# Attention beside experts on one core: two buffers of moved keys, filled at step 12 of the sequence before, and a different order in step 0

## The chip, the core and the metric

The kernel runs as one program on one core of a Trainium2 chip. The metric is device time in microseconds (us) of one execution, from the first to the last instruction and what lies around them. Every engine of the core (TensorE, VectorE, ScalarE, GpSimd, SyncE) runs an instruction stream of its own, and the streams meet at semaphores. In the profile TensorE is PE (its weight loads are PEld), VectorE DVE, ScalarE ACT, GpSimd POOL, and SyncE, which issues nearly all DMAs here, SP.

## What is computed

The input x has 8 sequences of 512 tokens with 512 features. Both stages are residual, with a layer norm before and after:

```python
x = x + layernorm(attention(layernorm(x)))
x = x + layernorm(experts(layernorm(x)))
```

Attention has 16 heads of 32 features for the queries and **one** head of keys and values that all of them share; it is causal, with biases:

```python
q = (h @ q_w.T + q_b).reshape(b, s, 16, 32)
k = h @ k_w.T + k_b                      # 32 features, shared by the 16 heads
v = h @ v_w.T + v_b
scores = einsum('bqhd,bkd->bhqk', q, k) / 32 ** 0.5      # then causal mask and softmax
out = einsum('bhqk,bkd->bqhd', attn, v).reshape(b, s, 512) @ o_w.T + o_b
```

The expert stage sends each token to 2 of 8 experts (gated, 352 features inside) and adds a shared expert (1408 features inside) under a sigmoid gate.

## The kernel before, in words

`build_layer` runs four parts one after another: `build_attention`, `build_routing`, `build_experts` (tokens sorted into places of 256) and `build_shared`. The change touches `build_attention` alone.

**Precision.** Products are made from pairs of float32r tiles, a high part and the rest (`low`), so a product of 512 features takes 12 matmuls (`split_product`, L400: 4 chunks by 3 passes). For the scores the parts are stacked along the contraction: `Qs` holds 3*32 rows per head (high, low, high of the queries), `KsS` the matching 96 rows of the keys (high, high, low) of one sequence. A second copy of the keys, `KsT`, has one more row of ones, so that the product with row 97 of `Qs`, the negated maxima, comes out shifted for the exponential.

**Order of the work.** There is no planner; each engine has its order written out in a function `turn(b)`, which handles sequence b in 16 steps s, one head of queries per step, in a software pipeline with lags. In step s of turn b TensorE does, in this order (L597 to L614):

- `query_scores(b, s)` (L423): four score products of head s against `KsS` and the mask (L434, L438) in three PSUM units. Before unit u it waits until DVE has reduced the head before to its maxima (`max_ready`). In step 0 it also waits for `kS_moved`, and in steps 0, 4, 8, 12 for `q_moved`.
- `rows_of_maxima(b, s)` (L579): transposes the maxima of the head before (L421). ACT copies the row out (`take_row`, L880) and SP moves it by DMA into row 97 of `Qs` (`move_row`, L343).
- `first_filler(b, s)` (L501): other dense work in the one bank `F_ps`. The chunks of the projected queries of sequence b+1 are made in steps 12, 13 and 15, chunk 3 in step 0 of the next turn (`Q_STEP`, L274). Other steps hold the output projection, the transposes of the input and the router.
- `begin_values` / `end_values`: products of the exponentials with ones or values (L458), a group of four heads at a time.
- `key_scores(n, h)` (L441, matmuls L451), two heads behind: transposed shifted scores against `KsT`, unit by unit, each waiting until ACT has taken the same unit of the head before (`pt_ready`). In steps 1 and 14 it stands before the values, in the others behind them.

**Step 0 is an exception**: `first_filler(b, 0)`, the projection of query chunk 3 (L403), stands ahead of `query_scores(b, 0)`. DVE mirrors it: it takes the low part of the filler's product (`low_q`, L637) before the third unit of maxima, as in the steps of `PAIRED` (2, 3, 9, 10); in all others after it.

ACT, in step s: exponentials of unit 0 of head s-3 (L869), `take_row`, the high part of a mixed group (L913), exponentials of units 1 and 2, the filler's high part (`high_q`, L837), then normalizations; steps 0 and 1 hold two each of `xn2` (L819) from b = 2 on. `high_q` precedes `low_q` of the same chunk; the next filler may begin when `low_q` is done (`qkv_lo`).

SP, in step s: from step 15 the first thing is the refill of `KsS` for sequence b+1: wait for `scores >= 3*H*(b+1)`, which is the last score product of sequence b, then three DMAs from `vk_h` (`move_k`, L320, issues L322), then `move_row`. `vk_h` itself is made in step 11 (`low_vk`, L624: ACT L828, DVE L630 and L632). `KsT` is moved in step 2 of turn b+1.

**Turns.** `turns` (L291) writes out turns 0 and 1, loops over 2 to 5 with a register (`Fori`), and writes out 6 to 9; the last two have no new sequence and drain the pipeline. Before turn 0 the first keys and chunks 0 to 2 of the queries are projected; chunk 3 of sequence 0 is made in step 0 of turn 0.

Of the kernel before, what the change touches and what calls it, by code (L numbers as in the profile page):

```python
# [26 lines left out]
P = 128  # L27
# [151 lines left out]
def build_attention(nc, x, wq, wvk, wo, wr, qb, vkb, ob, x1_out, xn_out, xnT_out, logits, idf, idb, mask, norm_constants):  # L179

    ctx = ExitStack()
    with ctx:
# [25 lines left out]

        QK = 3 * HD
        Qs = sb("Qs", [QK + 1, H, S], F32R)  # L210
        KsS = sb("KsS", [QK, S], F32R)
        KsT = sb("KsT", [QK + 1, S], F32R)
        V = sb("V", [P, QT, HD])
        ones_f = sb("ones_f", [P, QT, HD])
# [76 lines left out]
        block = ctx.enter_context(nc.Block())  # L291

        def turns(engine, turn):
            turn(0)
            turn(1)
            with engine.Fori(2, NB - 2) as b:
                turn(b)
            for b in range(NB - 2, NB + 2):
                turn(b)

        def seq(dram, b):
            return dram[bass.ds(b, 1)].rearrange("o p t d -> p (o t) d")
# [2 lines left out]
        def _(sp):  # L305
# [27 lines left out]
            sp.wait_ge(xT1_ps, C)  # L333
            sp.dma_start(x_in[:], seq(x, 1)).then_inc(x_in_s, 16)
            sp.wait_ge(qkv_lo, 1)
            move_k(0, KsS, kS_moved)
            move_k(0, KsT, kT_moved)
            spill_q(0, 0)
            spill_q(0, 1)
# [8 lines left out]
                    sp.dma_start(Qs[QK:QK + 1, h, :].bitcast(F32),  # L348
                                 row[:, h % 2, :].bitcast(F32)).then_inc(row_moved[h % 2], 16)

            def turn(b):
                for s in range(H):
                    if s == H - 1 and has(b + 1):
                        sp.wait_ge(scores, 3 * H * (b + 1))
                        move_k(b + 1, KsS, kS_moved)
                    move_row(b, s)
                    if s == 0 and has(b):
                        spill_q(b, 2)
                    if s == 1 and has(b):
                        move_q(b, 2)  # L360
                        spill_q(b, 3)
                    if s == 2 and has(b):
                        if has(b - 1):
                            sp.wait_ge(shifted, 3 * H * b)
                            move_k(b, KsT, kT_moved)
                        move_q(b, 3)
                    if s == 4 and has(b - 2):
                        sp.wait_ge(xT2_lo, C * (b - 1))
                        for half in range(2):
                            sp.dma_start(xnT_out[bass.ds(b - 2, 1), half].rearrange("o p c t -> p (o c) t"),  # L370
                                         xT[half][:].bitcast(F32)).then_inc(xnT_stored, 16)
                        sp.dma_start(seq(xn_out, b - 2), xn2[:]).then_inc(xn2_moved, 16)
                    if s == 6 and has(b - 1):
                        if has(b - 2):
                            sp.wait_ge(x1_ready, QT * (b - 1))
                        sp.dma_start(x_res[:], seq(x, b - 1)).then_inc(x_res_s, 16)
                    if s == 11 and has(b + 2):
                        sp.wait_ge(xT1_ps, C * (b + 2))
                        sp.dma_start(x_in[:], seq(x, b + 2)).then_inc(x_in_s, 16)
                    if s == 13 and has(b + 1):  # L380
                        spill_q(b + 1, 0)
                    if s == 14:
                        if has(b + 1):
                            move_q(b + 1, 0)
                            spill_q(b + 1, 1)
                        if has(b - 1):
                            sp.wait_ge(x1_ready, QT * b)
                            sp.dma_start(seq(x1_out, b - 1), y[:]).then_inc(x1_stored, 16)
                    if s == 15 and has(b + 1):
                        move_q(b + 1, 1)  # L390
# [7 lines left out]
        def _(pe):  # L398
# [21 lines left out]
                pe.wait_ge(max_ready, 3 * (H * n + h) + 3)  # L420
                nc.tensor.matmul(AV_ps[0:QT, 0:P], nmax[:, h % 2, :], idr[:], start=True, stop=True).then_inc(rows_ps, 1)  # L421

            def query_scores(b, s):  # L423
                if s == 0:
                    pe.wait_ge(kS_moved, 48 * b + 48)
                if s % HG == 0:
# [2 lines left out]
                for units in ((0,), (1, 2)):  # L429
                    for u in units:  # L430
                        if has(n):
                            pe.wait_ge(max_ready, 3 * (H * n + h) + u + 1)
                        for i, col in S_UNITS[u]:
                            nc.tensor.matmul(S_ps[u][:, col:col + (i + 1) * P], Qs[0:QK, s, i * P:(i + 1) * P],  # L434
                                             KsS[:, 0:(i + 1) * P], start=((i, col) == S_UNITS[u][0]), stop=False)
                    for u in units:
                        (i, col), k = S_UNITS[u][0], len(S_UNITS[u])
                        nc.tensor.matmul(S_ps[u][:, col + i * P:col + (i + k) * P], idb[:, 0, :],  # L438
# [155 lines left out]
                        pe.wait_ge(row_taken, H * head(b, s, 2)[0] + head(b, s, 2)[1] + 1)  # L594
                    transpose_maxima(n, h)

            def turn(b):  # L597
                for s in range(H):
                    if s == 0:
                        first_filler(b, s)  # L600
                    if has(b):
                        query_scores(b, s)
                    rows_of_maxima(b, s)
                    if s > 0:
                        first_filler(b, s)
                    n, h = head(b, s, 2)
                    if s in (1, 14) and has(n):
                        key_scores(n, h, head(b, s, 3))
# [10 lines left out]
        def _(dve):  # L619
# [168 lines left out]
                    if (s, at) == (15, 0):  # L788
                        x1_.guess(b - 1)

            def turn(b):
                for s in range(H):
                    maximum(b, s, 0)
                    norm_steps(b, s, 0)
# [1 line left out]
                    maximum(b, s, 1)  # L796
                    norm_steps(b, s, 1)
                    spread_inverses(b, s)
                    if s in PAIRED or s == 0:
                        first_low(b, s)  # L800
                        maximum(b, s, 2)
                        norm_steps(b, s, 2)
                        second_low(b, s)
                    else:
                        maximum(b, s, 2)
                        norm_steps(b, s, 2)
                        first_low(b, s)
# [8 lines left out]
        def _(act):  # L816
# [95 lines left out]
                        act.wait_ge(projected, QT * n)  # L912
                    nc.scalar.activation(OT[0][:, g, :], mixed_f[:], ACT.Copy).then_inc(OT_hi, 1)  # L913

            def turn(b):
                for s in range(H):
                    exponentials(b, s, 0)
                    take_row(b, s)
# [24 lines left out]
        def _(pool):  # L943
# [44 lines left out]
                pool.wait_ge(y_normed, QT * n + i + 1)  # L988
                nc.gpsimd.tensor_tensor(y[:, i, :], y[:, i, :], x_res[:, i, :], ALU.add).then_inc(x1_ready, 1)

            def turn(b):
                for s in range(H):
                    if s == 6 and has(b + 1):
                        norm[0].refine(b + 1)
# [849 lines left out]
```

## Time and profile before

| | us |
|---|---|
| median of 3 runs (lowest, highest) | 2149.88 (2144.54, 2150.34) |
| the profiled execution, its own time | 2153.74 |
| its span, first to last instruction | 2152.0 |
| PE busy in the span | 1973.5 (92%) |
| PEld, DVE, ACT, POOL busy | 1568.8, 1129.8, 781.6, 478.2 |
| mean granted TensorE clock | 0.943 of full |

The profiled execution is 3.9 us longer than the median of the three runs; its span is 1.7 us short of its own time. A row of a timeline has the start, the duration, the engine, line and operation, what is written from what, the shape and the count of merged instructions; in brackets, the idle time of the engine just before and what ended it. A "busy" matmul row shows that PE was occupied, not that it ran at its peak. [...]

### The profile page before, as it was taken

The page shows a single profiled execution, that of the slowest core. Times are in us where ns is not written, and L with a number is a line of the kernel's source. Part 1 is how long each engine was busy: PE and PEld are TensorE (multiplying, and loading weights), DVE is VectorE, ACT ScalarE, POOL GpSimd, SP SyncE. Part 2 cuts the span into 40 slices and gives each one's busy share as a digit, 9 for nine tenths or more (in the row PEclk, how much of TensorE's full clock was granted, in tenths as well). Part 3 has the DMA queues.
Part 4 walks back from the last instruction along what each step waited for, and adds up shares of the span by engine and source line. Part 5 has one row for each costly group of instructions (what it writes and reads, how often), then busy time and mean ns, then how long its engine had stood idle before and what let it go on. Part 6 is the DMA issues. An engine that isn't in the chain of part 4 may idle for free. (4 is left out here: it accounts for less than half of the span.)

```text
span 2152.0 us, 34973 instructions
## 1 busy us (share of the span) xinstructions
PE 1973.5 (92%) x11932; PEld 1568.8 (73%) x11932; DVE 1129.8 (52%) x2478; ACT 781.6 (36%) x1576; POOL 478.2 (22%) x1087
## 2 busy tenths in 40 slices
PE   5989999999999743899999999999999999999995
PEld 3665656656565422799999999978888888888884
DVE  4556656666565328677777657643433324333243
ACT  3445545455453410466666546432111111111111
POOL 1223324234241320211111112001113021130212
PEclk9799999999999765899999989999999999999998
DMA  5144353442533132566666657632123020230202
GB/s 173 51 114 127 117 174 106 147 143 109 176 98 126 50 113 95 195 237 236 235 235 235 240 188 268 243 113 69 37 81 118 19 97 31 86 117 19 97 24 94
DMA packets 114453, 281.47 MB, mean 131 GB/s; under 512 B 11680, under 2 KB 26272, under 8 KB 105024
## 3 DMA queue, kind: packets, MB, share of 16 engines
q1 hardware_dynamic: 103328, 244.18, 32.9%
q0 software_dynamic: 11040, 36.18, 5.0%
q8 instruction: 51, 0.84, 0.2%
q14 instruction: 34, 0.28, 0.0%
HBM read 198.79 MB, written 78.12 MB: 129 GB/s over the span
## 5 line engine op out<-in xcount | busy, mean ns | idle before, releaser
L1257 PE MATMUL ex_bank<-ex_xT,ex_gu 128*128 128x256 f32 (+12 forms) x2808 | 358.0, 284 | 1.0 <-DVE ex_xT L1421 1.0
L1257 PEld LDWEIGHTS ex_bank<-ex_xT,ex_gu 128*128 128x128 f32 (+1 forms) x2808 | 344.1, 185 | 4.9 <-issue 1.4
L1289 DVE TENSOR_TENSOR sh_silu<-sh_silu,sh_bank 128x512 f32<-128x512 f32 x88 | 60.6, 688 | 457.4 <-ACT sh_silu L1282 451.1
L1282 ACT ACTIVATE sh_silu<-sh_bank 128x512 f32<-128x512 f32 x88 | 52.6, 598 | 591.4 <-PE sh_bank L1257 546.1
L1257 PE MATMUL sh_bank<-sh_xT,sh_gate 128*128 128x512 f32 x1056 | 256.2, 392 | 5.2 <-DVE sh_dn L1704 5.2
L677 DVE TENSOR_REDUCE at_nmax<-at_bank 128x1 fp32r<-128x384 f32 (+3 forms) x512 | 222.6, 476 | 61.2 <-PE at_bank L438 60.7
L1269 PE MATMUL sh_bank<-sh_dn,sh_act 128*128 128x512 f32 x1056 | 254.3, 390 | 0.0
L1257 PE MATMUL sh_bank<-sh_xT,sh_up 128*128 128x512 f32 x1056 | 253.7, 389 | 0.0
L1257 PEld LDWEIGHTS sh_bank<-sh_xT,sh_gate 128*128 128x128 f32 x1056 | 199.8, 189 | 47.3 <-issue 5.6
L869 ACT ACTIVATE at_PT<-at_bank 128x512 f32<-128x512 f32 (+1 forms) x384 | 184.2, 506 | 125.7 <-PE at_bank L451 101.0
L1269 PEld LDWEIGHTS sh_bank<-sh_dn,sh_act 128*128 128x128 f32 x1056 | 197.6, 188 | 43.7 <-DVE sh_act L1298 2.9
L1257 PEld LDWEIGHTS sh_bank<-sh_xT,sh_up 128*128 128x128 f32 x1056 | 198.4, 188 | 41.3
L1269 PE MATMUL ex_bank<-ex_dn,ex_act 128*128 128x512 f32 (+1 forms) x666 | 165.2, 401 | 0.6 <-issue 0.6
L451 PE MATMUL at_bank<-at_Qs,at_KsT 97*128 97x512 f32 (+3 forms) x512 | 127.1, 363 | 27.4 <-ACT at_PT L869 18.5
L1269 PEld LDWEIGHTS ex_bank<-ex_dn,ex_act 128*128 128x128 f32 (+1 forms) x666 | 124.7, 192 | 27.7 <-issue 1.5
L973 POOL TENSOR_SCALAR_AFFINE_SELECT at_PT<-at_PT 128x384 f32<-128x384 f32 x128 | 66.9, 522 | 294.4 <-ACT at_PT L869 294.3
L1349 DVE TENSOR_TENSOR ex_gu<-ex_gu_in,ex_gu 128x704 fp32r<-128x704 f32 x156 | 131.3, 884 | 1.2 <-PEq L1018 0.6
L451 PEld LDWEIGHTS at_bank<-at_Qs,at_KsT 97*128 97x128 f32 x512 | 86.7, 203 | 58.3 <-ACT at_PT L869 22.5
L434 PE MATMUL at_bank<-at_KsS,at_Qs 96*128 96x384 f32 (+3 forms) x512 | 123.0, 349 | 6.8 <-DVE at_nmax L677 5.7
L1345 ACT ACTIVATE ex_gu<-ex_gu_in 128x704 fp32r<-128x704 f32 x156 | 115.5, 801 | 27.2 <-DMA ex_dn_in<-dn_in 27.2
L1289 DVE TENSOR_TENSOR ex_silu<-ex_silu,ex_bank 128x256 f32<-128x256 f32 (+15 forms) x117 | 45.9, 392 | 142.9 <-ACT ex_silu L1282 142.8
L403 PE MATMUL at_bank<-at_xT,at_wq 128*128 128x512 f32 x384 | 95.5, 398 | 9.7 <-DVE at_q_h L637 9.2
(228 smaller groups left out, 2653.8 us busy)
## 6 DMA issues: line engine op xcount, KB each, us to landing
ex_gu_in<-gu_in SPq DMA_DIRECT2D x39, 1408.0 KB
at_Qs<-q_dram SPq DMA_DIRECT2D x96, 256.0 KB, 4.0
ex_dn_in<-dn_in SPq DMA_DIRECT2D x39, 512.0 KB
ys<-sh_yk SPq DMA_DIRECT2D x35, 512.0 KB, 2.9
q_dram<-at_q_h SPq DMA_DIRECT2D x64, 256.0 KB, 3.2
xnT<-at_xT SPq DMA_DIRECT2D x16, 1024.0 KB, 5.0
sh_xT<-xnT SPq DMA_DIRECT2D x16, 1024.0 KB
at_x_in<-x_in SPq DMA_DIRECT2D x8, 1024.0 KB, 5.1
```

The costliest lines, as they stand in the source:

```text
L403: last = nc.tensor.matmul(out, w[i][:, c, cols], xT[j][:, c, :], start=(n == 0), stop=(n == 3 * C - 1))
L434: nc.tensor.matmul(S_ps[u][:, col:col + (i + 1) * P], Qs[0:QK, s, i * P:(i + 1) * P], KsS[:, 0:(i + 1) * P], start=((i, col) == S_UNITS[u] ...
L451: last = nc.tensor.matmul(T_ps[tb][:, col:col + w], KsT[:, j * P:(j + 1) * P], Qs[:, h, j * P:S], start=((j, col) == tiles[0]), stop=((j, ...
L677: last = nc.vector.tensor_reduce(nmax[:, s % 2, i:i + 1], S_ps[u][:, col:col + (i + 1) * P], AX_X, ALU.max, negate=True)
L869: nc.scalar.activation(PT[g % 2][:, h % HG, TFROM[tb]:TFROM[tb] + TW[tb]], T_ps[tb][:, 0:TW[tb]], ACT.Exp).then_inc(pt_ready, 1)
L973: nc.gpsimd.affine_select(out=diagonals, in_=diagonals, compare_op=ALU.is_ge, fill=0.0, base=0, pattern=[[0, QT - 1], [1, P]], channel_mul ...
L1257: last = self.nc.tensor.matmul(self.gate_up_ps[c % 2][which][0:m, 0:w], cols(i, k), self.xT[j][:, k, 0:w], start=(step == 0), stop=(step = ...
L1269: last = self.nc.tensor.matmul(self.out_ps[i][:], self.act[c % 2][j][0:m, i * P:(i + 1) * P], weights(k), start=(c == 0 and step == 0), st ...
L1282: nc.scalar.activation(silu[c % 2][0:m, 0:w], gate_up_ps[c % 2][0][0:m, 0:w], ACT.Silu).then_inc(s["silu_ready"], 1)
L1289: nc.vector.tensor_tensor(silu[c % 2][0:m, 0:w], silu[c % 2][0:m, 0:w], gate_up_ps[c % 2][1][0:m, 0:w], ALU.mult).then_inc(s["product"], 1)
L1345: self.nc.scalar.activation(self.piece(q, r, 0), self.piece(q, r), ACT.Copy).then_inc(self.hi, 1)
L1349: self.nc.vector.tensor_tensor(self.piece(q, r, 1), self.piece(q, r), self.piece(q, r, 0).bitcast(F32), ALU.subtract).then_inc(self.lo, 1)
```

## The change

`KsS` becomes two buffers, used by the sequence's parity r. SP no longer fills one in step 15 behind the last scores; it fills the other one in step 12, behind that step's `move_row` and a wait for `low_vk(b+1)`. In step 0 PE does the scores and the row of maxima first and the projection of query chunk 3 after them, as in the other steps, and DVE takes all three units of maxima before `low_q`. The parity must be known when the program is written, so the loop now holds two turns in its body: turns 0 and 1 are written out, `Fori(1, 3)` runs turns (2, 3) and (4, 5), and 6 to 9 are written out.

```diff
-        KsS = sb("KsS", [QK, S], F32R)
+        KsS = [sb(f"KsS{r}", [QK, S], F32R) for r in range(2)]
...
         def turns(engine, turn):
-            turn(0)
-            turn(1)
-            with engine.Fori(2, NB - 2) as b:
-                turn(b)
+            turn(0, 0)
+            turn(1, 1)
+            with engine.Fori(1, NB // 2 - 1) as pair:
+                turn(2 * pair, 0)
+                turn(2 * pair + 1, 1)
             for b in range(NB - 2, NB + 2):
-                turn(b)
+                turn(b, b % 2)
...
-            move_k(0, KsS, kS_moved)
+            move_k(0, KsS[0], kS_moved)
...
-            def turn(b):
+            def turn(b, r):
                 for s in range(H):
-                    if s == H - 1 and has(b + 1):
-                        sp.wait_ge(scores, 3 * H * (b + 1))
-                        move_k(b + 1, KsS, kS_moved)
                     move_row(b, s)
+                    if s == 12 and has(b + 1):
+                        sp.wait_ge(qkv_lo, 5 * b + 6)
+                        move_k(b + 1, KsS[1 - r], kS_moved)
...
                             nc.tensor.matmul(S_ps[u][:, col:col + (i + 1) * P], Qs[0:QK, s, i * P:(i + 1) * P],
-                                             KsS[:, 0:(i + 1) * P], start=((i, col) == S_UNITS[u][0]), stop=False)
+                                             KsS[r][:, 0:(i + 1) * P], start=((i, col) == S_UNITS[u][0]), stop=False)
...
-            def turn(b):
+            def turn(b, r):
                 for s in range(H):
-                    if s == 0:
-                        first_filler(b, s)
                     if has(b):
-                        query_scores(b, s)
+                        query_scores(b, s, r)
                     rows_of_maxima(b, s)
-                    if s > 0:
-                        first_filler(b, s)
+                    first_filler(b, s)
...
-                    if s in PAIRED or s == 0:
+                    if s in PAIRED:
                         first_low(b, s)
```

## Rows read from the trace of the kernel before

**Rows 1.** The windows view, the attention part: window, length, busy of PE, PEld, DVE, ACT, POOL, then PEclk, DMA share, GB/s.
```profile
40.00:764.00 724.00, 672.55 (x4804) 439.39 (x4803) 432.10 (x1016) 333.48 (x727) 235.11 (x610) 0.94 0.38 122
```
**Rows 2.** The waits view, PE from 44 to 764: total us, times, longest.
```profile
PE at_bank L403 <- DVE at_q_h L637: 6.8, 7, 1.0
PE at_bank L451 <- DMA at_KsT<-at_vk_h: 5.8, 7, 1.4
```
**Rows 3.** Timeline of PE from turn 4 into turn 5.
```profile
461.38 0.81 PE L451 MATMUL at_bank<-at_Qs,at_KsT 97*128 97x512 f32 x4
463.18 3.06 PE L403 MATMUL at_bank<-at_xT,at_wq 128*128 128x512 f32 x12 [1.00 <-DVE at_q_h L637]
466.07 0.40 PE L434 MATMUL at_bank<-at_KsS,at_Qs 96*128 96x384 f32 x2
...
466.97 0.45 PE L451 MATMUL at_bank<-at_Qs,at_KsT 97*128 97x512 f32 x1
468.05 0.67 PE L451 MATMUL at_bank<-at_Qs,at_KsT 97*128 97x128 f32 x3 [0.63 <-ACT at_PT L869]
...
470.00 0.38 PE L434 MATMUL at_bank<-at_KsS,at_Qs 96*128 96x256 f32 x1 [0.68 <-DVE at_nmax L677]
...
470.78 0.49 PE L451 MATMUL at_bank<-at_Qs,at_KsT 97*128 97x512 f32 x1 [0.20 <-ACT at_PT L869]
```
**Rows 4.** Timeline of ACT at the same place.
```profile
461.65 0.69 ACT L837 ACTIVATE at_q_h<-at_bank,at_qb 128x512 fp32r<-128x512 f32 x1 [1.29 <-PE at_bank L403]
...
467.25 0.27 ACT L880 ACTIVATE at_row<-at_bank 4x128 fp32r<-4x128 f32 x1 [4.43 <-PE at_bank L421]
...
468.17 0.66 ACT L837 ACTIVATE at_q_h<-at_bank,at_qb 128x512 fp32r<-128x512 f32 x1
...
470.15 0.57 ACT L869 ACTIVATE at_PT<-at_bank 128x512 f32<-128x512 f32 x1
```
**Rows 5.** Timeline of DVE: the low part of query chunk 2, in step 15.
```profile
462.38 0.75 DVE L637 SCALAR_TENSOR_TENSOR at_q_h<-at_bank,at_qb,at_q_h 128x512 fp32r<-128x512 f32 x1 [2.26 <-ACT at_q_h L837]
```
**Rows 6.** The same view, step 11 of turn 4.
```profile
442.06 0.68 DVE L632 TENSOR_TENSOR at_vk_h<-at_vk,at_vk_h 64x512 fp32r<-64x512 f32 x1
```
**Rows 7.** Timeline of SP's issues in turn 4: steps 12 and 13, then 14, then 15.
```profile
443.39 3.97 SPq L348 DMA_DIRECT2D at_Qs<-at_row  x2
...
454.63 1.27 SPq L330 DMA_DIRECT2D at_Qs<-q_dram  x3
...
458.69 3.03 SPq L322 DMA_DIRECT2D at_KsS<-at_vk_h  x3
```
**Rows 8.** The tile view of KsS, time from issue to landing of its 24 DMAs.
```profile
DMA to landing us min/median/max: 2.0/4.5/5.3
```
**Rows 9.** Timeline of PE from turn 0 into turn 1.
```profile
114.22 3.02 PE L403 MATMUL at_bank<-at_xT,at_wq 128*128 128x512 f32 x12 [0.92 <-DVE at_q_h L637]
...
122.33 0.67 PE L451 MATMUL at_bank<-at_Qs,at_KsT 97*128 97x128 f32 x3 [0.55 <-ACT at_PT L869]
```
**Rows 10.** Timeline of PE at the start of turn 0.
```profile
39.64 3.00 PE L403 MATMUL at_bank<-at_xT,at_wq 128*128 128x512 f32 x12 [2.43 <-DVE at_q_h L637]
43.69 0.47 PE L434 MATMUL at_bank<-at_KsS,at_Qs 96*128 96x384 f32 x2 [1.04 <-DMA at_Qs<-q_dram]
...
47.05 0.25 PE L421 MATMUL at_bank<-at_idr,at_nmax 128*4 128x128 f32 x1
```
**Rows 11.** Timeline of PE: the same 32 value matmuls in step 1 of turns 4 and 7.
```profile
385.55 2.36 PE L458 MATMUL at_bank<-at_PT,at_ones_f 128*32 128x512 f32 x32
...
648.11 4.50 PE L458 MATMUL at_bank<-at_PT,at_ones_f 128*32 128x512 f32 x32
```
**Rows 12.** The windows view, steps 15 to 1 around turn 7, columns as in rows 1.
```profile
636.00:652.00 16.00, 13.72 (x74) 8.11 (x76) 4.83 (x10) 7.54 (x15) 5.65 (x21) 0.80 0.73 216
```
**Rows 13.** The DMA view, queue of instruction packets (count, MB): 298 to 570 (in the loop), 576 to 700.
```profile
q8 instruction: 2, 0.03, 0.1%
...
q8 instruction: 7, 0.11, 0.4%
```

More of the change, by code:

```diff
@@ L421, in transpose_maxima, with query_scores @@
                 nc.tensor.matmul(AV_ps[0:QT, 0:P], nmax[:, h % 2, :], idr[:], start=True, stop=True).then_inc(rows_ps, 1)
-            def query_scores(b, s):
+            def query_scores(b, s, r):
                 if s == 0:
@@ L789, in norm_steps, with turn @@
                         x1_.guess(b - 1)
-            def turn(b):
+            def turn(b, r):
                 for s in range(H):
@@ L913, in high_mixed, with turn @@
                     nc.scalar.activation(OT[0][:, g, :], mixed_f[:], ACT.Copy).then_inc(OT_hi, 1)
-            def turn(b):
+            def turn(b, r):
                 for s in range(H):
@@ L989, in add_residual, with turn @@
                 nc.gpsimd.tensor_tensor(y[:, i, :], y[:, i, :], x_res[:, i, :], ALU.add).then_inc(x1_ready, 1)
-            def turn(b):
+            def turn(b, r):
                 for s in range(H):
```

## The prediction

> **What bounds the kernel now.** I read the windows by stage first. In the attention part PE is busy 672.6 of 724 us at a mean granted clock of 0.94 [rows 1]: TensorE sets the pace there, and what is to be won is its 51 idle us and the time at the lower clock. No other engine is above 61%. The part after it starts when attention ends, so what attention saves should pass to the end whole. Then the waits of PE: two of its groups come once per turn, 6.8 us on `low_q` in 7 waits of at most 1.0, and 5.8 us on the move of `KsT` in 7 waits [rows 2]. The change is about the first, so I read the timelines from turn 4 into turn 5.
>
> The reader is to see four stops of PE there [rows 3]. The key scores of head 13 end near 462.2 (461.38+0.81). The projection of chunk 3 begins at 463.18, 1.00 late, because it waits for `low_q` of chunk 2, which ends at 463.13 [rows 5]. The scores of head 0 start only at 466.07. The row of maxima of head 15 thus reaches ACT late: ACT has been idle 4.43 before `take_row` at 467.25 [rows 4]. Behind that copy stand exponentials of head 13, so PE stops 0.63; `low_q` of chunk 3 stands ahead of a maximum on DVE, so PE stops 0.68 at 470.00; then 0.20 at 470.78, where the key scores of head 15 wait for ACT [rows 3].
>
> **The new order of step 0, PE, DVE and ACT.** From the key scores of head 13 on, with durations of these rows. The scores and the row take 0.90 (466.07 to 466.97), so they run 462.2 to 463.1, in the hole before 463.18. They need three things. The maxima of head 15, reduced in step 15, are there. The queries: their three DMAs are issued at 454.63 to 455.9 [rows 7]; even with the longest landing of a move of keys, 5.3 [rows 8], that is 461.2. The keys are discussed below. The projection starts where it did, 463.18, and ends its issue at 466.07. ACT takes the row early, in its 4.43 us of idleness, and does the exponentials of head 13 there; the 0.63 stop goes. All maxima of head 0 are done before `low_q`; the 0.68 stop goes. PE then does the key scores of head 14 (0.81) and the scores and row of head 1 (0.90) by 467.8.
>
> **What is late next** is ACT. `high_q` of chunk 3 can begin when the projection ends (463.18+3.06=466.24), instead of at 468.17 behind the copy and the exponentials. Behind it stand two normalizations and the exponential of head 14, unchanged. From `high_q` to the key scores of head 15 it was 470.78-468.17=2.61 [rows 3, 4]; now 466.24+2.61=468.85. PE waits about 1.0 there, in one piece, and the gain is 470.78-468.85=**1.9**. The norm's factors from GpSimd come early enough: nothing there follows this order. This holds for the six boundaries into turns 2 to 7: 6*1.9=11.3. Into turn 1 there are no such normalizations: scores in the hole, projection at 114.22 as before, its issue ends 117.1, key scores and scores to 118.8, then the copy and two exponentials (1.1 from the row to the second unit, as 466.89 to 468.05); the second unit starts near 119.9 instead of 122.33 [rows 9]: 2.4. Together **-13.7**. After step 1 PE is full again and every later chain (the row to SP, `KsT`) hangs on PE's own steps, so the shift stays. The KsT wait stays too: its DMAs follow the row of head 1.
>
> **The second buffer and SP.** The three moves go from step 15 (458.69 to 461.7, landed up to 5.3 later, 466) [rows 7, 8] to step 12. Without this the new order would wait for them. In step 12 they follow the row at 443.39 and a wait for `low_vk`, done at 442.06+0.68=442.7 [rows 6, 7], so SP waits for nothing. The three issues hold SP up to 3.0 us; the next row comes 3.4 us after the first (two rows span 3.97, one takes 0.6) and is needed a step later (724/128=5.7 us): cost 0. Were the first cover gone, that row would be late by at most 3.0, less than the step. In step 15 the row of head 14 goes some 2 us earlier; it was not waited for. `KsT` moves as before. DMA traffic is the same. The added buffer costs space only. PE's reads of either buffer cost the same.
>
> **The start.** Here the old order was the better one. The projection of chunk 3 ran at 39.64 while the first queries were on their way, and the scores began at 43.69, waiting for them [rows 10]. Now the scores begin at 43.69 and the projection lies bare behind them. The row of head 0 came at 47.05; now 43.69+0.90+2.89+0.90=48.4, a loss of 1.4, if the clock stays up. But PE is then idle from 37.2 to 43.7 instead of 2.4 and 1.0. After such a stop the clock may be at its lower level, where the same 32 matmuls take 4.50 us against 2.36 [rows 11], 1.9 times. Then it is 1.9*4.7=8.9, ending at 52.6, a loss of 5.6. SP's moves of chunk 2 stand behind this row, so the loss is passed on. I take **+4.0**, nearer to the low clock, since so long a stop precedes; ends 1.4 and 5.6.
>
> **The loop.** The body has two turns. In 272 us inside the loop two packets of 16 KB of instructions are fetched, in 124 us of written-out turns seven [rows 13]: the body now stays in the engines' memories and its return costs nothing that is seen. A body twice as long may not stay. It would then be fetched as the written-out turns are, which show no stop at fetches, except that the one return (turn 3 to 4) jumps to code that is not there. No row prices such a jump; the nearest is the landing of a small DMA, 2.0 to 5.3 [rows 8]. Ends 0 and 5.3, taken **+2.0**, once, because PE no longer has a hole at that place.
>
> [...]
>
> **The clock.** [...] There the 32 value matmuls cost 4.50 instead of 2.36 [rows 11], so all six cost at most 6*2.1=12.8. The change takes PE's idle time at a boundary from 2.5 (1.00+0.63+0.68+0.20) to about 1.0, and leaves that in one piece. One boundary, into turn 4, kept its clock with the same stops. So the fall is a near thing, and I take half of it away: **-6**; ends 0 and -12.8.
>
> **Sum**: -13.7+4.0+2.0-6=-13.7. Against the profiled execution, 2153.7 becomes 2140.0 (span 2138.3). That execution is 3.9 above the median of the runs shown; against the median 2149.9 becomes **2136.2**.
>
> **Rivals.**
> - *The clock holds everywhere* (0.15): all of the 12.8 returns and the start costs 1.4, the loop 0: -13.7+1.4-12.8=-25, 2125. For it: PE's density at a boundary becomes that of other steps. Against: the 1.0 in one piece.
> - *The gain is given back at the start and to the clock* (0.15): start 5.6, return 5.3, clock nothing: -2.8, 2147. For it: six of seven falls at present.
> - *The change does not do what it says* (0.04): scores in step 0 find another late input, queries or the mask unit, and the hole stays: 2149 to 2151. Against it: the landing worked out above.
> - *Slower: fetching code* (0.04). With a doubled body every one of the five engines jumps to code it does not hold, and they stand in a chain (PE, DVE, ACT, SP, back to PE), so the stops add up. Five of 5.3 are 26; with clock 0 and start 4.0 it is -13.7+4.0+26=+16, 2166. It decides from about 16 us of fetching stops. Against: in written-out turns fetches hide.
>
> **The numbers.** About 0.3%, 6.4 us, is what a measurement of this kernel can tell from no change. The forecast with its own range of 2129 to 2143 has 0.62 and is faster; the clock rival too (0.15); of the second rival 0.02. Faster 0.79, same 0.17, slower 0.04. The range, 2125 to 2148, leaves out the slower rival and the tails.
>
> **What would show it.** In the profile after: at a boundary the scores of head 0 directly behind the key scores of head 13; ACT's wait before `take_row` gone; no PE wait on DVE maxima there, and one of about 1.0 on ACT exponentials before the key scores of head 15. The L403 wait on `low_q` shrinks from 6.8 to under 1. At the start the projection lies behind 43.7. More instruction packets between turns 2 and 5; a stop of several engines at the return from turn 3 to 4. It is wrong if the boundaries keep their length, or the start costs over 6, or the granted clock is low in places where it was full.

## The result, and the profile after

| | before | after |
|---|---|---|
| median (lowest, highest), us | 2150.34 (2144.54, 2154.41) | 2138.74 (2135.79, 2139.76) |
| runs of each | 7 | 7 |
| the profiled execution, own time | 2153.74 | 2135.84 |
| its span | 2152.0 | 2134.1 |
| mean granted clock of TensorE | 0.943 | 0.949 |

The ratio is 0.9946, with a 95% interval of 0.9933 to 0.9960: 11.6 us faster, where 2136.2 was forecast. The two profiled executions lie 17.9 apart, since that of before is 3.4 above its median and that of after 2.9 below. Another 1.6 us of the 17.9 is scatter ahead of attention: the first store of queries is issued at 34.95 before and at 33.37 after.

The page of after, its first lines and its instruction queues:

```profile
span 2134.1 us, 34901 instructions
PE 1957.1 (92%) x11932; PEld 1566.4 (73%) x11932; DVE 1128.9 (53%) x2478; ACT 782.0 (37%) x1576; POOL 478.4 (22%) x1087
q8 instruction: 69, 1.13, 0.2%
q14 instruction: 50, 0.41, 0.1%
```

The windows view over the attention part, where PE's busy time was 672.55 at a clock of 0.94 [rows 1]:

```profile
40.00:764.00 724.00, 663.40 (x4828) 442.04 (x4828) 437.36 (x1031) 336.83 (x731) 242.87 (x628) 0.95 0.39 122
```

PE is busy 9.2 us less over a few more matmuls, and in the whole span 16.4 us less over the same 11932: the same work took less time. The waits of PE from 44 to 764 (total us, times, longest):

```profile
PE at_bank L452 <- ACT at_PT L867: 19.9, 19, 5.0
PE at_bank L452 <- DMA at_KsT<-at_vk_h: 6.5, 7, 1.4
PE at_bank L435 <- issue: 3.6, 1, 3.6
PE at_bank L452 <- DMA at_Qs<-at_row: 3.4, 2, 2.8
```

The group of 6.8 us on `low_q` [rows 2] is gone, the wait for `KsT` has stayed, and a single wait of 3.6 on "issue" is new. The timeline of PE from turn 5 into turn 6 is that of [rows 3], one turn later:

```profile
542.57 0.81 PE L452 MATMUL at_bank<-at_Qs,at_KsT 97*128 97x512 f32 x4
543.21 0.40 PE L435 MATMUL at_bank<-at_KsS,at_Qs 96*128 96x384 f32 x2
...
544.37 3.02 PE L404 MATMUL at_bank<-at_xT,at_wq 128*128 128x512 f32 x12
547.23 0.81 PE L452 MATMUL at_bank<-at_Qs,at_KsT 97*128 97x512 f32 x4
...
550.15 1.21 PE L452 MATMUL at_bank<-at_Qs,at_KsT 97*128 97x512 f32 x4 [1.22 <-ACT at_PT L867]
```

The scores of head 0 follow the key scores of head 13 at once, and of the four stops one of 1.22 is left. From the key scores of head 13 to those of head 15 it is 550.15-542.57=7.58 us, against 470.78-461.38=9.40 [rows 3]: 1.82 less. This stretch is called the boundary below; without its stop it takes 7.58-1.22=6.36. ACT at the same place:

```profile
544.31 0.27 ACT L878 ACTIVATE at_row<-at_bank 4x128 fp32r<-4x128 f32 x1 [0.29 <-PE at_bank L422]
...
547.43 0.69 ACT L835 ACTIVATE at_q_h<-at_bank,at_qb 128x512 fp32r<-128x512 f32 x1 [2.11 <-PE at_bank L404]
548.02 1.51 ACT L817 ACTIVATE at_xn<-at_y,at_bias_x,at_rstd_x 128x512 f32<-128x512 f32 x2
549.43 0.58 ACT L867 ACTIVATE at_PT<-at_bank 128x512 f32<-128x512 f32 x1
```

Its wait ahead of `take_row` fell from 4.43 [rows 4] to 0.29. Now it waits 2.11 for the projection, and the two normalizations stand between `high_q` and the exponential that PE wants.

**The clock behind the boundaries** is read from windows of 16 us that begin at the key scores of head 15 (columns as in rows 1, the clock third from the end). Before, into turns 1, 2, 3, 5 and 7:

```profile
122.00:138.00 16.00, 13.34 (x127) 7.30 (x128) 8.07 (x18) 4.75 (x12) 3.55 (x7) 0.89 0.56 145
205.00:221.00 16.00, 14.84 (x116) 7.46 (x120) 8.82 (x19) 7.64 (x18) 2.06 (x5) 0.79 0.57 158
295.00:311.00 16.00, 14.90 (x126) 7.24 (x124) 8.69 (x18) 7.58 (x17) 2.82 (x6) 0.81 0.54 144
...
470.00:486.00 16.00, 14.76 (x128) 7.21 (x128) 9.56 (x21) 8.27 (x19) 3.15 (x6) 0.89 0.58 157
...
645.00:661.00 16.00, 13.99 (x100) 7.32 (x101) 7.68 (x18) 6.78 (x15) 1.54 (x4) 0.74 0.58 160
```

After, at the same five places:

```profile
122.00:138.00 16.00, 13.23 (x143) 7.58 (x147) 10.31 (x23) 5.43 (x14) 3.73 (x8) 1.00 0.57 145
201.00:217.00 16.00, 14.05 (x139) 7.54 (x140) 9.84 (x22) 8.94 (x20) 3.58 (x7) 1.00 0.56 145
286.00:302.00 16.00, 13.79 (x124) 7.44 (x124) 9.42 (x19) 7.88 (x18) 3.55 (x7) 0.89 0.56 145
...
463.00:479.00 16.00, 13.76 (x124) 7.20 (x124) 9.59 (x20) 8.05 (x19) 3.58 (x7) 0.89 0.57 146
...
634.00:650.00 16.00, 14.75 (x145) 8.53 (x145) 8.92 (x19) 8.85 (x20) 3.58 (x7) 1.00 0.57 145
```

The other two boundaries read 1.00 (turn 4) and 0.89 (turn 6) before, and 1.00 and 1.00 after. In windows of 1 us the clock reads 1.00 or 0.50, but for those in which it changes (before, into turn 2: 1.00 in each from 200 to 205, 0.50 in each from 206 to 211). So a mean of 0.89 over 16 us is (1-0.89)*16/0.5=3.5 us at the lower level. Over the seven windows that makes 31.7 us before and 7.0 after. At the return from turn 3 to 4 after has a fall of its own, ahead of its window: from 366 to 382 the mean is 0.79, 6.7 us, of which some 1.4 lie under PE's stop there. These windows begin behind the boundary and do not show a fall inside it.

**The start of turn 0**, PE, against [rows 10]:

```profile
42.02 0.77 PE L435 MATMUL at_bank<-at_KsS,at_Qs 96*128 96x384 f32 x2 [6.36 <-DMA at_Qs<-q_dram]
...
43.66 4.87 PE L404 MATMUL at_bank<-at_xT,at_wq 128*128 128x512 f32 x12
...
50.75 0.50 PE L435 MATMUL at_bank<-at_KsS,at_Qs 96*128 96x384 f32 x2 [1.33 <-DVE at_nmax L675]
```

PE stands 6.36 in one piece, and the projection behind it takes 4.87 instead of 3.00. **The return of the loop** from turn 3 to 4, PE and then ACT:

```profile
369.90 0.79 PE L435 MATMUL at_bank<-at_KsS,at_Qs 96*128 96x384 f32 x2 [3.57 <-issue]
...
371.71 4.67 PE L404 MATMUL at_bank<-at_xT,at_wq 128*128 128x512 f32 x12
...
369.27 0.60 ACT L867 ACTIVATE at_PT<-at_bank 128x512 f32<-128x512 f32 x1 [2.78 <-issue]
```

Between 280 and 550 the first instruction queue moves 18 packets, 0.29 MB, where two were moved inside the loop before [rows 13], and the second 15, 0.12 MB. One of the first and two of the second lie inside PE's stop, from 366.33 to 369.90. The boundary at the return takes 13.61 us (365.52 to 379.13) where the others take 7.5 to 7.6: 3.57 for the stop, and some 2.5 for the work that ran at the lower clock.

**Where the time went**, from one issue of SP to the same one a turn later (the store of x in step 14): before 89.05, 89.24, 86.55, 88.12, 87.32, 87.41 us; after 84.82, 86.15, 90.78, 87.11, 84.09, 79.38. Five intervals are shorter by 1.0 to 8.0. The third holds the return and is 4.2 longer. The sum is 527.69 against 512.33, 15.4 less. From the last store of attention to the end it is 1370.6 before and 1370.3 after: all of the gain is in attention, as was forecast.

### The profile page after: what moved, and what is told of

The parts are those of the page before. It is cut to its first block and busy times, and to the rows that moved or that the text cites. A ratio compares the mean times of both kernels' runs of the same rounds, so it can differ in the third digit from the quotient of the medians.

```text
span 2134.1 us, 34901 instructions
## 1 busy us (share of the span) xinstructions
PE 1957.1 (92%) x11932; PEld 1566.4 (73%) x11932; DVE 1128.9 (53%) x2478; ACT 782.0 (37%) x1576; POOL 478.4 (22%) x1087
## 5 line engine op out<-in xcount | busy, mean ns | idle before, releaser
L452 PE MATMUL at_bank<-at_Qs,at_KsT 97*128 97x512 f32 (+3 forms) x512 | 120.9, 353 | 30.4 <-ACT at_PT L867 19.9
L166 POOL TENSOR_TENSOR sh_t<-sh_t 128x4 f32<-128x4 f32 x40 | 8.0, 200 | 433.1 <-DVE sh_t L153 430.6
```

Source lines behind the costliest of these rows:

```text
L166: self.nc.gpsimd.tensor_tensor(out, in0, in1, op).then_inc(self.newton, 1)
L452: last = nc.tensor.matmul(T_ps[tb][:, col:col + w], KsT[:, j * P:(j + 1) * P], Qs[:, h, j * P:S], start=((j, col) == tiles[0]), stop=((j, ...
```

## The experiments

**Everything written out.** The loop goes, and with it the return; the order of step 0 is after's.

```diff
-            turn(0, 0)
-            turn(1, 1)
-            with engine.Fori(1, NB // 2 - 1) as pair:
-                turn(2 * pair, 0)
-                turn(2 * pair + 1, 1)
-            for b in range(NB - 2, NB + 2):
+            for b in range(NB + 2):
                 turn(b, b % 2)
```

> The changed kernel with all ten attention turns written out, so that no engine jumps back; nothing else differs. Theory (the 3.57 us stop of TensorE and the 2.78 us stop of ScalarE at the return from turn 3 to 4, which the profile puts down to issue, are the fetch of code that is no longer held, and the fall of the clock behind it comes from this stop): both stops are gone, no attention boundary is longer than the others, and the time falls by 3.6 for the stop and up to 3 more for the clock, to 2132 to 2135. Rival (the stop is something else that happens once at this place, such as a late DMA or a register wait): it stays, and the time stays at 2138 to 2140. Second rival (written-out code pays at each fetch): small stops appear in turns 2 to 5 and eat the gain.

Measured: 2135.06 (2133.78 to 2137.90), ratio 0.9932 (0.9915 to 0.9950). No wait of PE or ACT on issue is left in attention. The waits of PE there:

```profile
PE at_bank L447 <- ACT at_PT L862: 19.8, 19, 4.9
...
PE at_bank L447 <- DMA at_KsT<-at_vk_h: 4.0, 7, 1.4
```

The intervals are 83.68, 85.53, 83.92, 85.62, 85.76, 81.42: in sum 6.4 shorter than after's. The part behind attention, from its last store of x to the end, gives 5 of that back (1375.3 against 1370.3); by the ratios 0.0014, 3 us, are left of it. A turn with no fall of the clock behind its boundary takes 83.7 to 83.9, one with a fall of 3.5 us (a window of 0.89) 85.5 to 85.8: the fall costs about 1.8. The 5 us behind attention were not expected; later experiments come back to them.

**The old start.** Only in the first step of all, PE takes the projection first again.

```diff
                 for s in range(H):
+                    first_ever = s == 0 and isinstance(b, int) and b == 0
+                    if first_ever:
+                        first_filler(b, s)
                     if has(b):
                         query_scores(b, s, r)
                     rows_of_maxima(b, s)
-                    first_filler(b, s)
+                    if not first_ever:
+                        first_filler(b, s)
```

> The changed kernel with one exception: in step 0 of turn 0 TensorE makes the projection of query chunk 3 ahead of the scores, as before the change. Theory (the new order loses 4 us at the start because the projection no longer lies under the arrival of the first queries): the row of maxima of head 0 comes 2 to 4 us earlier, and the time falls by 3 to 4, to about 2135. Rival (the loss is only moved: the first turn is limited by the DMAs of queries and rows, which wait for nothing of this): the time stays within 1 us of 2138.7.

Measured: 2133.04 (2131.78 to 2136.72), ratio 0.9926 (0.9908 to 0.9944), which is 0.0020 or 4.3 us below after's ratio. By the two profiles, from the first store of queries to the first store of x it is 153.05 us instead of 156.89: 3.8 less. The start had cost 3.8 to 4.3.

**The order alone**, in before: one buffer, keys moved in step 15, loop of one turn.

```diff
                 for s in range(H):
-                    if s == 0:
-                        first_filler(b, s)
                     if has(b):
                         query_scores(b, s)
                     rows_of_maxima(b, s)
-                    if s > 0:
-                        first_filler(b, s)
+                    first_filler(b, s)
```

(DVE's `if s in PAIRED or s == 0` becomes `if s in PAIRED`.)

> The kernel before with the new order of step 0 alone (TensorE and VectorE); one buffer of moved keys, filled in step 15, and the loop of one turn. Theory (the second buffer is what lets the scores run in the hole): the scores of head 0 now wait for the keys, which land near 4 us after the key scores of head 13 end; TensorE stops 3 to 4 us at each of seven boundaries, of which the new order gives back 1.9, so the time is 5 to 15 us above the kernel before, with the start loss of 4 in it: 2160 to 2175. Rival (the keys land early enough, and the buffer was not needed): it equals the changed kernel less the stop at the return, near 2134.

Measured: 2152.28 (2148.03 to 2155.56) over 12 runs, ratio 1.0008 (0.9996 to 1.0021). PE's wait group, its timeline into turn 4, and the clock from 385 to 401:

```profile
PE at_bank L434 <- DMA at_KsS<-at_vk_h: 17.1, 6, 3.9
...
377.00 0.60 PE L434 MATMUL at_bank<-at_KsS,at_Qs 96*128 96x384 f32 x2 [3.62 <-DMA at_KsS<-at_vk_h]
...
378.62 3.92 PE L403 MATMUL at_bank<-at_xT,at_wq 128*128 128x512 f32 x12
...
385.00:401.00 16.00, 14.71 (x144) 8.17 (x145) 9.88 (x21) 8.89 (x20) 3.57 (x7) 1.00 0.55 144
```

The wait for the keys comes, six times and 2.0 to 3.9 long, and takes the gain away: the early move is what the order needs. But hardly a loss followed, and the expected time was far too high. The six boundaries into turns 2 to 7 take 71.8 us together, against 56.2 before, 15.6 more: 17.1 of waits for keys, 7.2 of waits for ACT, 38.2 of work (6*6.36), and 9.3 that the work runs longer. The start costs its 4; the boundary into turn 1 gives 2.7. What pays for most of this is the clock behind the boundaries. In windows of 16 us from the key scores of head 15 all six read 1.00, where the same six had 28.2 us at the lower level before, worth 14.1. But the clock has not stayed up: it falls inside each boundary. The projection right behind each wait is slow (3.92 to 4.56 in the six places, for 3.0). In windows of 1 us around that at 377.00 the granted clock is 1.00 during the whole wait, then 0.62, 0.50, 0.50 and 0.68 from 377 to 381, and 1.00 again. So each of the six has one fall of 3.4 us, all of it on work, and the 9.3 is its price. The sum is 15.6+4.0-2.7-14.1=2.8, and measured by the ratio is 1.7 (-0.9 to 4.5).

**Buffers and loop alone.** After's two buffers and its loop of two turns, with the old order and the keys moved in step 15.

```diff
-        KsS = sb("KsS", [QK, S], F32R)
+        KsS = [sb(f"KsS{r}", [QK, S], F32R) for r in range(2)]
...
-            with engine.Fori(2, NB - 2) as b:
-                turn(b)
+            with engine.Fori(1, NB // 2 - 1) as pair:
+                turn(2 * pair, 0)
+                turn(2 * pair + 1, 1)
```

> The changed kernel with the old order of step 0 and the keys moved in step 15 as before; what is left of the change is two buffers and the loop with two turns in its body. Theory (a body of two turns is fetched anew and its one return stops TensorE and ScalarE for the fetch): one stop with the releaser issue at the return from turn 3 to 4, some 1 us shorter than in the changed kernel because 1.0 us was idle there anyway, and a time 2 to 6 us above the kernel before, 2152 to 2156. Rival (the stop belongs to the new order, whose scores follow at once): no such stop, and the time of before, 2150.

Measured: 2150.86 (2146.33 to 2153.97) over 12 runs, ratio 1.0009 (0.9995 to 1.0022). PE's waits and the return:

```profile
PE at_bank L404 <- issue: 3.6, 1, 3.6
...
373.25 5.48 PE L404 MATMUL at_bank<-at_xT,at_wq 128*128 128x512 f32 x12 [3.57 <-issue]
```

The stop of 3.57 belongs to the loop of two turns, whatever the order, and again one instruction packet of the first queue and two of the second lie inside it, from 369.68 to 373.25. Here it swallows one old stop of 1.0. The boundary at the return takes 14.45 us instead of 9.41, 5.0 more, while by the ratio the whole is only 1.9 longer (-1.1 to 4.7). In the profiled execution, the fastest of the twelve, the clock fell behind only three boundaries besides the return, where before's profile has six; why is open. Two buffers bring nothing by themselves.

**The order alone, seen from the other side.** The written-out program has the two buffers and the move in step 12; this takes from it only the order, on PE and DVE.

```diff
                 for s in range(H):
+                    if s == 0:
+                        first_filler(b, s)
                     if has(b):
                         query_scores(b, s, r)
                     rows_of_maxima(b, s)
-                    first_filler(b, s)
+                    if s > 0:
+                        first_filler(b, s)
```

> Two buffers, the keys moved in step 12, all turns written out, but the old order of step 0 on TensorE and VectorE. Theory (moving the keys earlier is worth nothing by itself, SP's three issues in step 12 are free, and written-out turns cost nothing): the boundaries show the four stops of before, 1.0, 0.63, 0.68 and 0.20, and the time is that of before, 2148 to 2152. Rival (part of the gain comes from the earlier move, since SP is free in step 15 and the landing traffic is away from the boundary): the time lies 3 or more below before, under 2147.

Measured: 2154.44 (2153.22 to 2158.31) over 12 runs, ratio 1.0031 (1.0019 to 1.0043). The old stops stand in it as they did:

```profile
374.23 3.01 PE L399 MATMUL at_bank<-at_xT,at_wq 128*128 128x512 f32 x12 [0.92 <-DVE at_q_h L633]
...
380.93 0.38 PE L430 MATMUL at_bank<-at_KsS,at_Qs 96*128 96x256 f32 x1 [0.69 <-DVE at_nmax L673]
```

The time was expected at that of before and is 0.0031, 6.6 us, above it. Most of that is the 5 us that this program, written out like the first, loses behind attention (1375.4 from the last store of x). Against the written-out program with the new order (0.9932) the order is worth 0.0099, 21 us, net of its loss at the start. So the early move alone gives nothing, the order alone gives nothing, and the two together some 25 us at seven boundaries. 13.3 of them are the stops (six boundaries of 9.29 became 7.52, and the first, 8.84, became 6.15). The clock has the rest: in windows of 16 us from the key scores of head 15, the seven boundaries read 0.89, 0.79, 0.79, 0.79, 0.89, 0.89, 0.79 with the old order (37 us at the lower level) and 1.00, 1.00, 0.89, 1.00, 0.89, 0.89, 0.89 with the new (14 us).

**A hint on the loop's closing branch.** The changed kernel and its loop stay; on each engine the loop is built with `hint_back_edge=True`.

```diff
-            with engine.Fori(1, NB // 2 - 1) as pair:
+            with nc.Fori(1, NB // 2 - 1, engines=[engine.engine], hint_back_edge=True) as pair:
```

> [...] Theory (the stop at the return is the fetch of the loop's first instructions): TensorE's stop of 3.6 with the releaser issue goes or is under 1, and the time is that of the written-out turns, about 2135. Rival (the stop is not the fetch, or the hint acts on something else): the stop stays at 3.5, time 2138.7.

Measured: 2133.85 (2130.54 to 2136.83), ratio 0.9928 (0.9909 to 0.9947), 0.0018 or 3.9 us below after's. At the return:

```profile
367.42 0.80 PE L452 MATMUL at_bank<-at_Qs,at_KsT 97*128 97x512 f32 x4
368.06 0.40 PE L435 MATMUL at_bank<-at_KsS,at_Qs 96*128 96x384 f32 x2
...
369.23 3.04 PE L404 MATMUL at_bank<-at_xT,at_wq 128*128 128x512 f32 x12
```

The 3.57 is gone and the projection keeps its clock (a fall of 3.4 us comes some 8 us later, at 377), with the part behind attention at its 1370.2. Since the hint is all that differs, the stop is shown to hang on the jump back. That the jump waits for code is the author's reading. What the traces show of it are the packets: between 280 and 550 the second instruction queue moves 3 where it moved 15, the first 18 as in after. From 366.33 to 369.90, where after stops with three packets inside, there is one here, of the first queue, and PE works on. How the hint does it is not shown.

**Written out, and the old start.** The first two edits together.

> The changed kernel with all turns written out and the projection of chunk 3 ahead of the scores in turn 0 alone: the edits of the first two experiments together. Theory (the stop at the return and the start are two separate losses, about 3.7 and 4 to 5.7 us): they add up, and the time is 2130 to 2132. Rival (both are the same clock luck seen twice): no lower than the better of the two, 2133.

Measured: 2132.32 (2129.23 to 2134.98), ratio 0.9918 (0.9899 to 0.9938). The two gains nearly add (0.9946-0.0014-0.0020=0.9912). Where the 5 us behind attention go is seen in the waits of the shared expert, of this kernel (860 to the end):

```profile
PE sh_bank L1254 <- issue: 3.8, 4, 1.0
PEld sh_bank L1254 <- issue: 11.1, 5, 5.6
```

With the old start but the loop of turns kept, there is one wait of 5.6 on PEld, and none on PE.

**The normalizations first.** The stop left at a boundary is ACT's, behind two normalizations (L817); here ACT does them before `high_q`, in its 2.11 us of waiting, and the other two in step 1 as ever.

```diff
+                        if s == 0 and has(b - 2):
+                            act.wait_ge(xn2_moved, 16 * (b - 1))
+                            for i in range(0, 2):
+                                normalize(xn2, y, 2, b - 2, i, xn_ready)
...
-                    if s in (0, 1) and has(b - 2):
-                        if s == 0:
-                            act.wait_ge(xn2_moved, 16 * (b - 1))
-                        for i in range(2 * s, 2 * s + 2):
+                    if s == 1 and has(b - 2):
+                        for i in range(2, 4):
```

> The kernel of the fifth experiment with one more edit: in step 0 ScalarE does the two normalizations ahead of the high part of query chunk 3 instead of behind it. Theory (ScalarE's chain high part, two normalizations, exponential is what TensorE now waits for by 1.2 us at each boundary, while ScalarE is idle before it): the wait before the key scores of head 15 shrinks to about 0.4, GpSimd's factors being the next to be late; six boundaries give 4 us or so, and the clock falls less often; the time is 2124 to 2128. Rival (GpSimd's factors come later than ScalarE is free, and the high part then waits behind the normalizations): the wait stays at 1.2 and the time with it, 2131.

Measured, on top of the preceding kernel: 2122.42 (2119.91 to 2124.78), ratio 0.9876 (0.9855 to 0.9897). PE into turn 4, and ACT:

```profile
366.98 1.21 PE L447 MATMUL at_bank<-at_Qs,at_KsT 97*128 97x512 f32 x4 [0.58 <-ACT at_PT L866]
...
364.25 1.52 ACT L816 ACTIVATE at_xn<-at_y,at_bias_x,at_rstd_x 128x512 f32<-128x512 f32 x2 [1.39 <-POOL at_bias_x L176]
```

The stop of 1.2 became 0.58, and the intervals are 83.04, 83.34, 83.30, 83.44, 83.43, 77.79. The first five sum to 416.6, against 424.6 in the kernel it was built on (83.70, 85.61, 83.94, 85.64, 85.73): 8.1 went, while the stops shrank by 0.64 a turn, 3.2. The remaining 4.9 fits the three falls of about 1.8 each that are gone: the five intervals are alike. The fourth fall, into turn 7, is gone too, and the sixth interval is 3.6 shorter (81.40 before this edit). In return the first store of x comes 1.6 us later after the first store of queries (154.68 for 153.07): in turn 1, which the edit does not touch, the window from 122 to 138 reads 0.89 instead of 1.00. The order alone and the two experiments that follow show the same fall, and why it comes is open.

**All of it with the loop kept**: hint, old start, normalizations first.

> The three edits that helped, on the changed kernel with its loop kept: the hint for the closing branch, the projection of chunk 3 ahead of the scores in turn 0 alone, and the two normalizations of step 0 ahead of the high part. Theory (each removes a loss of its own: the stop at the return, 4 us at the start, 0.6 to 0.7 at six boundaries with part of the clock's falls; and the loop's program does not have the 5 us that the written-out programs lose after attention): 2116 to 2119. Rival (the 5 us after attention are no matter of the written-out turns): 2121 to 2123, as the sixth experiment.

Measured: 2123.25 (2120.78 to 2125.66), ratio 0.9883 (0.9868 to 0.9898). The part behind attention is back at 1370.4, as expected, but the expected time was missed: the intervals are 83.89, 84.43, 83.97, 85.40, 84.02. The first four, in the loop, are 0.7 to 2.0 longer than the same turns written out, and the fifth, written out in both, 0.6; the clock behind the boundaries into turns 2 to 7 reads 1.00. SP's issues scatter; by PE's key scores of head 13 the five turns are 0.40, 1.35, 0.51, 1.15 and 0.69 longer, 4.1 in all. PE's waits for `KsT` are 7.3 instead of 4.0, and 1.5 and 1.4 of them stand in turns 3 and 5, the second of each pair, where the written-out program waits 0.4. So the loop costs in its turns about what the written-out program loses behind attention. Part of it is the wait for `KsT`; what makes that later, and the rest, is open.

**The written-out turns with the hint on the shared expert's loop**, which also has two turns.

```diff
-            with engine.Fori(0, NB // 2 - 1) as pair:
+            with nc.Fori(0, NB // 2 - 1, engines=[engine.engine], hint_back_edge=True) as pair:
```

> The kernel of the sixth experiment (all attention turns written out) with the hint on the loop of two turns in the shared expert. All written-out programs show four new stops of TensorE with the releaser issue in that loop, one to each turn up to the fourth, and end 5 us later behind attention than the programs with a loop. Theory (the longer program before it shifts the loop's code against the blocks in which instructions are fetched, so that code is missing at a branch): with the hint these stops go and the time is 2117 to 2118. Rival (code is missing inside the body, not at the branch): the stops stay and the time with them, 2122.

Measured: **2115.32** (2114.72 to 2117.85), ratio 0.9845 (0.9830 to 0.9860), 33 us below before. The waits of the shared expert in it:

```profile
PEld sh_bank L1256 <- issue: 5.6, 1, 5.6
```

The four stops on PE are gone and the part behind attention takes 1370.4, 3.8 less than in the kernel that it was built on. By the ratios it is 0.0031, 6.7 us, faster than that one, and faster than was expected; the two intervals leave room for the difference. Between 1602 and 1999, inside this loop, the first instruction queue moves 19 packets in the kernel it was built on, 2 in after, and none here. Why code ahead of this loop brings the packets and the stops is not shown: the hint tells only that they hang on its branch. This version beats both kernels.

## Why the prediction was right, and by which steps

- **Boundaries, -13.7.** Right in place, kind and size. Measured 1.82 for 1.9 (a stop of 1.22 for 1.0 on exponentials, where it was named), and into turn 1, where the key scores of head 15 come at 122.00, 7.11 behind those of head 13 instead of 9.84, 2.7 for 2.4: 6*1.82+2.73=13.7.
- **The keys.** That the order needs the early move was right in direction: alone it gains nothing. The landing "466" put the wait at about 3; it was 2.0 to 3.9. What was wrong is the price of it expected for the order alone, 10 to 25 us more than before, in which the clock behind the boundaries was held to fall as before; it fell once and for 3.4 us at each, inside the boundary, and behind it no more.
- **SP's moves, 0.** Right: in step 12 the three issues take 1.83 at 348.22, and the row behind them follows at 350.92 on the normal pace.
- **The start, +4.0.** Right: 3.8 by the profile, 4.3 by the ratios. The projection ran at the low clock (4.87 for 3.00) behind the long stop, as in the upper of the two cases, but 5.6 was not reached.
- **The loop's return, +2.0.** This term was sized too small, and it is the one that failed in part. The stop is 3.57 on PE, inside the ends of 0 and 5.3, and the fall of the clock behind it (4.67 for 3.02) comes on top: removing both gave 3.9. The cost had been bounded by a landing and the clock at that place forgotten, although in before it was the one boundary that kept its clock. The slower rival needed the stops of five engines to add up; they overlap (PE 3.57 and ACT 2.78, ending within 0.7 us of each other). That a body of two turns would be fetched anew was the author's estimate from [rows 13], and the packets bear it out: 18 of the first queue between 280 and 550, and three of both queues inside PE's stop of 3.57.
- **The clock, -6.** Right by the medians: -11.6 is -13.7+3.8+3.6 and a rest of -5.3, the fall at the return included. In the two profiled executions the rest is larger: -17.9 less 1.6 of scatter is -16.3, which leaves -10.0. The time of work at the lower level went from 31.7 to 7.0, plus 5.3 at the return, so 19.4 us less, and half of that is 9.7. The written-out pair of programs, old order against new, puts the clock at about 25-13.3=12 us. So the size of this term is settled no better than between 5 and 12: the interval of the ratio alone is 2.9 us to either side. The forecast took half of a bound because the fall is a near thing, and that this half meets the medians is partly luck. The six falls that the bound counts are there: six of the seven boundaries read below 1.00 in the windows of before, with 0.50 at the lower level, and the 16 us around the start of turn 7 had 0.80 [rows 12]. The bound itself was too low: 6*2.1=12.8 counted one group of value matmuls per boundary, while the 31.7 us at the lower level cost about 16. That only some boundaries would keep the clock was right: four of seven do (turns 1, 2, 6, 7), and the return lost the one it had. The three others kept theirs once the turns were written out and the normalizations moved.

The range of 2125 to 2148 and the likeliest case's own, 2129 to 2143, both hold the result. The rivals in which the clock holds everywhere or the gain is given back would have needed 2125 and 2147; neither happened.

## What to carry to other kernels

Where a wait that stands at the same place in every turn is removed, look next at what the engine behind it still does first: here 0.6 us of stop at each of six boundaries and four falls of the clock hung on two normalizations that could stand elsewhere in their own queue. Price a stop of PE with what the clock does behind it, which here added 5 to 12 us to 13.7. And look for a fall inside the stretch as well as behind it. And when a loop body grows, or code is written out, read the waits on "issue" at every later return of any loop, and try a hint on the branch before anything is rebuilt.

## What the runs showed of the hardware that was not expected

- The one return of the loop whose body was doubled stopped PE for 3.57 us, in two orders of the work alike, and ACT for 2.78 and 2.95, with three instruction packets inside each of PE's stops; with the hint on the branch neither stop is there, and the second instruction queue moves 3 packets instead of 15 between 280 and 550.
- Code ahead of a loop changed that loop: with the turns of attention written out, the unchanged loop of the shared expert got four stops (3.8 to 4.1 us on PE, and 11.1 to 11.4 instead of 5.6 on PEld) and 5 us of time, and 19 or 20 packets of the first instruction queue between 1602 and 1999 instead of 2; with the hint on it there are none, PE has no such stop and the 5 us are gone.
- The clock fell for longer behind four scattered stops of 2.5 us together (37 us over seven of seven boundaries in the written-out program with the old order, 3.5 or 6.8 at each) than behind one stop of 2.0 to 3.9 us (3.4 us at each of six, in the order alone), which slowed the projection right behind it (3.92 to 4.56 for 3.0) and left the steps after it at full clock.
- In the order alone, a stop of 3.62 us kept a granted clock of 1.00 to its end, and the fall began with the work behind it; at the return in after it began 1.4 us before the stop of 3.57 ended.
- A turn in the loop (after) took longer than the same turn with everything written out and the same clock behind its boundary (1.00 in turn 2, 0.89 in turn 5): by PE's key scores of head 13, turn 2 took 84.54 against 83.99 and turn 5 86.42 against 85.62.
